# Decoder layer on one core: scatters paced by quarters, value bias prepared later, residual before the combine weights

## The reference

```
x = layernorm(x + attn(x))            # causal
x = layernorm(x + xattn(x, ctx))      # V = ctx @ Wv + bv, out = context @ Wo + bo
x = layernorm(x + moe(x))             # top 2 of 8, y = sum of weight * expert(x)
```

## Time and profile before

| | |
|---|---|
| median of 3 runs | 1257.66 us (1256.6 to 1260.25) |
| the profiled execution | 1263.13 us, its span 1261.4 us |
| PE busy | 1059.1 us (84% of the span) |
| DVE busy | 806.9 us (64%) |
| ACT busy | 580.3 us (46%) |
| POOL busy | 266.1 us (21%) |
| mean granted clock of PE | 0.922 of full speed |

### The profile page before, as it was taken

The page is one execution under the profiler, slowest core; times in us unless marked ns, Lnnn a source line. Parts: engine busy times, 40 slices in busy tenths (PEclk is TensorE's granted clock), DMA queues, the critical chain, the costliest instruction groups (busy, mean ns, idle before and its releaser), DMA issues.

```text
span 1261.4 us, 29339 instructions
## 1 busy us (share of the span) xinstructions
PE 1059.1 (84%) x10925; PEld 787.2 (62%) x10925; DVE 806.9 (64%) x1955; ACT 580.3 (46%) x937; POOL 266.1 (21%) x309
## 2 busy tenths in 40 slices
PE   4799999999988999997988899868439999999930
PEld 2465665656666666665656566545329999999920
DVE  3677787777788887776767676655534444444447
ACT  1366666666655565644436354545212222222214
POOL 1034222232222200002020201120422222222210
PEclk8899999999999999999898988888559999999975
DMA  6005635536440001001010100010147676777654
GB/s 260 27 28 176 197 125 175 172 117 206 141 117 28 11 18 44 10 10 45 10 45 10 46 11 23 16 37 2 58 134 213 209 219 210 217 214 212 203 225 195
DMA packets 94650, 139.27 MB, mean 110 GB/s; under 512 B 11217, under 2 KB 68945, under 8 KB 93105
## 3 DMA queue, kind: packets, MB, share of 16 engines
q1 hardware_dynamic: 87888, 114.98, 29.1%
q0 software_dynamic: 6624, 22.42, 4.6%
HBM read 76.56 MB, written 60.29 MB: 108 GB/s over the span
## 4 chain that ended last, share of the span: by engine, by line
PE 67%; DVE 17%; issue 8%; another core or an unknown queue 3%; ACT 2%; SPq 2%; DMA 2%; DVEq 0%; ACTq 0%; POOLq 0%
PE PS L814 10%; PE PS L825 10%; PE PS L551 9%; PE PS L572 8%; PE PS L521 6%; PE PS L629 4%; DVE part L1108 4%; PE PS L625 4%; PE PS L670 3%; PE PS L643 2%; PE PS L696 2%; PE PS L708 1%; PE PS L803 1%; PE PS L528 1%
## 5 line engine op out<-in xcount | busy, mean ns | idle before, releaser
L1108 DVE TENSOR_REDUCE part<-PS 128x6 f32<-128x768 f32 (+1 forms) x256 | 269.9, 1086 | 92.9 <-PE PS L528 59.8
L891 ACT ACTIVATE pT<-PS 128x768 f32<-128x768 f32 (+1 forms) x256 | 220.8, 915 | 111.8 <-PE PS L551 89.2
L551 PE MATMUL PS<-big 32*128 32x256 f32 (+1 forms) x2048 | 136.4, 380 | 21.0 <-issue 15.7
L572 PE MATMUL PS<-pT,vaug 128*32 128x256 f32 (+1 forms) x2048 | 129.3, 371 | 22.4 <-DVE y L1242 16.1
L1567 POOL TENSOR_SCALAR_AFFINE_SELECT pT<-pT 128x512 f32<-128x512 f32 x128 | 81.6, 638 | 311.4 <-ACT pT L891 307.3
L814 PEld LDWEIGHTS PS<-oT,big 128*128 128x128 f32 x1136 | 140.1, 194 | 5.4 <-ACT oT L1002 1.8
L814 PE MATMUL PS<-oT,big 128*128 128x128 f32 x1136 | 140.8, 278 | 1.0 <-ACT oT L1002 1.0
L551 PEld LDWEIGHTS PS<-big 32*128 32x128 f32 x2048 | 98.3, 189 | 65.0 <-issue 63.2
L825 PE MATMUL PS<-w2s,qkn 128*128 x568 | 134.4, 380 | 0.0
L902 ACT ACTIVATE oT<-PS 128x256 f32<-128x256 f32 x128 | 49.0, 383 | 174.9 <-PE PS L572 148.7
L1002 ACT ACTIVATE oT<-PS 128x256 f32<-128x256 f32 x71 | 27.2, 383 | 189.9 <-PE PS L803 189.9
(11 more groups left out here) (169 smaller groups left out, 1646.5 us busy)
## 6 DMA issues: line engine op xcount, KB each, us to landing
big<-w SPq DMA_DIRECT2D x71, 512.0 KB
xs_dram<-zrow SPq DMA_DIRECT2D x24, 1496.0 KB, 9.3
oT<-xs_dram SPq DMA_DIRECT2D x71, 136.0 KB
xin<-xT SPq DMA_DIRECT2D x16, 256.0 KB, 2.8
w2s<-w POOLq DMA_DIRECT2D x1, 4096.0 KB, 15.3
xb<-x SPq DMA_DIRECT2D x16, 256.0 KB, 11.3
xin<-ctxT SPq DMA_DIRECT2D x16, 256.0 KB, 2.8
big<-p_dram SPq DMA_DIRECT2D x4, 1024.0 KB, 7.9
```

The lines of the kernel that those rows point to most:

```text
L551: ins = pe.matmul(o, keys, a[r0:r1, 0, g, q0:T], start=True, stop=True)
L572: ins = pe.matmul(o[PADDED * i:PADDED * (i + 1), q0:T], vaug[:, n % 4, kt, head(g, i), :], pT[:, k % 2, i, kt * T:kt * T + T - q0], start= ...
L891: act.activation(pT[:, k % 2, 2 * half:2 * half + 2, 0:wide], src, ACT.Exp).then_inc((exp_a, exp_b)[half], 1)
L1108: dve.tensor_reduce(dst, src, AX.X, ALU.max, negate=True).then_inc((max_a, max_b)[half], 1)
```

## The change

1. `turn_bias` and `take_bias` move from q = 1 to q = 6, `fold_bias` from q = 2 to q = 7, `add_folded` from q = 5 to q = 8.
2. `residual` of a block moves from the start of the quarter r = 0 to the end of the quarter before it (r = 3), behind `lay_out` and ahead of `combine_weights`.
3. `scatter` on POOL waits, in every quarter in which PE computes scores, until the scores of that quarter are done, before it issues the quarter's two indirect DMAs.

```diff
@@ PE
                 if q == 0:
                     prepare_gains()
-                elif q == 1:
+                elif q == 6:
                     turn_bias()
-                elif q == 2:
+                elif q == 7:
                     fold_bias()
@@ DVE
                 if r == 0:
-                    residual(block_at(q, PROJECT_AT + 1))
                     take_ranks(routed_at(q, PLACE_AT))
...
                     lay_out(block_at(q, LAY_AT))
+                    residual(block_at(q, PROJECT_AT))
                     combine_weights(routed_at(q, RANK_AT))
                 if q == 0:
                     prepare()
-                elif q == 1:
+                elif q == 6:
                     take_bias()
-                elif q == 5:
+                elif q == 8:
                     add_folded()
@@ POOL, scatter
                     ends = nt * TOPK if q == QUARTERS - 1 else min(2 * j + 2, nt * TOPK)
+                    u = group_at(q, SCORE_AT)
+                    if u is not None:
+                        pool.wait_ge(scores_pe, NG * u[0] + u[1] + 1)
                     for c in range(2 * j, ends):
```

## The result

The median went from 1257.47 us (1256.6 to 1260.25, four runs) to 1218.47 us (1215.94 to 1220.28, four runs): ratio 0.9685, 95% interval 0.9662 to 0.9708. The profiled execution took 1220.28 us, its span 1218.5 us, granted clock 0.944.

A forecast was written before the change was run, and what follows sets the result against it. Bound by PE (67% of the chain) and DVE (17%), plus PE's start wait and late reports during scatter bursts. 1263.1 - 8.0 (start) - 33.5 (gate) + 3.6 (residual) = 1225.2 profiled, 1219.7 as median; range 1210 to 1245.

The forecast's parts named there:

- The late reports come with indirects in a row: Cross-attention, five batches: POOL's bursts of eight scatters hold PE's reports; bursts cost 38.5 us with the slower clock.
- B: Scatters: reports not held by the burst, or only in a profiled execution; gate saves nothing, 1253 us; chance 0.11.
- A: Paced scatters: each pair holds 1.6 us on the path in three quarters; gate saves 14.5, 1239 us; chance 0.12.
- C: Paced scatters: reports held in each of four quarters, 3 us a pair; slower, 1275 us; chance 0.05.
- The sum: Whole kernel: 1263.1 - 8.0 - 33.5 + 3.6 = 1225.2 profiled; 5.5 off for the median gives 1219.7 us.
- Size of the gate: Paced scatters in five batches: 6.7 us saved per batch, 33.5 in all; bounds 38.5 and 14.5.
- 7.7 us a burst: Quarters r = 1 and 2 with scatters: 7.7 us longer, some 5.4 late reports, the rest PE's clock at 0.50.
- The pairs: Paced scatters: nothing for four in a row in r = 0 and 1; 0.5 us each in r = 2 and 3.
- The start: Kernel start: PE's 8.99 us wait for late loads goes, first maxima at 31.4 instead of 39.76; 8.0 us saved.
- The residual: Routing quarters: residual ahead of `combine_weights` loses cover, 4 x 0.3 + 1.2 + 1.2 = 3.6 us; bounds 0 and 5.
- the two terms of 1.2: Residual, routing quarters at 831.89 and 881.91: combine weights no longer run while DVE waits; 1.2 us lost in each.
- The signs named: First maxima 31.4; paired scatters, no remote wait over 1.5 before 860, r = 1 and 2 together 15 to 16, clock near 1.00.

The follow-up runs named there:

- the first comparison: The whole change against the kernel before, four runs each: 1257.47 to 1218.47 us, ratio 0.9685.
- chips 6 and 8: Chip 6: change with one scatter a quarter, 1216.01 us (before 1258.33). Chip 8: moved bias, one scatter a quarter, residual in old place, 1218.35 (before 1260.37).
- chips 7, 2 and 9: Kernel before, unchanged: 1214.40 us on chip 7, 1220.90 on chip 2, 1219.11 on chip 9; parts, spacings and the whole change were run beside it.
- chip 9: The whole change against the kernel before: 1210.74 us beside 1219.11, ratio 0.9935; moved bias alone 1206.11, ratio 0.9912.
- chip 2: Kernel before, unchanged, 1220.90 us; whole change 1212.44, with one scatter a quarter 1211.28, with four in r = 0 and four in r = 2 1214.74.
- the residual alone: Only the residual moved behind `lay_out`, against the kernel before on chip 7: 1215.11 us, ratio 1.0018.
- the single scatters: Whole change with one indirect a quarter instead of two for batches ending with blocks 17 to 25: 1216.01 us on chip 6, 1211.28 on chip 2.

## Why the prediction was right, step by step

**The late reports come with indirects in a row**: right in the first comparison, on chips 6 and 8 too by their times and by the "remote" waits of the kernels run there, but only half of the story. On chips 7, 2 and 9 the same bursts delay nothing. The prediction took the 38 us for a property of the kernel. It weighed B at 0.11 and priced it at 1253; B's outcome came true in another form: on those three chips the gate is worth nothing, and the whole change 0.9935, 8 us. Had the comparison been made there, the forecast of 38 us less would have been wrong by 30. The forecast needed, without knowing it, a comparison where late reports are there, as in its trace; in that much it was lucky. B's other half, that only a profiled execution has the holds, does not fit: the four runs beside the profiled one took 1256.6 to 1260.25 too. Of rivals A and C neither appeared. What the record lacks is a part alone on a chip with late reports; that the gate and not another part gave the 30 us there is read from where the time went.

**The sum.** 1219.7 against 1218.47 is closer than its parts, and that is luck. The sum for the profiled execution was 1225.2, and it took 1220.28, 4.9 less. By q = 101 the gain was 11.3 instead of 8.0, and behind q = 134 another 1.5 came that no term has. The medians agree because 5.5 us were taken off for the distance of the profiled execution to the median; in the kernel after that distance is 1.8.

**Size of the gate.** The forecast was 33.5 less the residual's 3.6, so 29.9. From q = 101 to 134 the gain is (251.33 + 12.14) - (225.46 + 7.94) = 30.1; the residual's first 0.3 and second 1.2 fall outside this stretch, so 31.4 is what was forecast for it. Term by term: 7.7 us a burst held the late reports and something else. Without late reports the same burst of the kernel before takes 596.17 - 587.94 = 8.23 from r = 1 to r = 2, as a block without scatters does (511.05 - 502.82); by the table the bursts cost 27.6 / 4 = 6.9 and 7.2. The rest of the 7.7 is there without them too, in PE's clock. Three windows (us, busy time of PE, PEld, DVE, ACT and POOL, granted clock) over the stretch from the maxima of r = 2 to those of r = 3: the first batch in after, then the first and the second batch in after on chip 9:

```profile
584.09:591.98 7.89, 7.89 (x69) 5.14 (x69) 5.81 (x14) 3.87 (x6) 1.94 (x2) 0.81 0.15 48
```

```profile
586.50:594.49 7.99, 7.99 (x69) 5.17 (x68) 5.82 (x14) 3.86 (x6) 1.93 (x2) 0.79 0.17 49
644.29:650.72 6.43, 6.43 (x69) 4.56 (x68) 5.83 (x15) 3.87 (x6) 1.94 (x2) 1.00 0.20 59
```

The granted clock of 0.50 of the earlier trace rows is gone, but the 1.00 that was expected everywhere is about 0.8 in this stretch in some batches, which then takes 7.9 to 8.0 us against 6.43 in the earlier trace rows: in all four of the kernel after, in one of four in the same kernel on chip 9, and in two of four in the kernel before on chip 2. PE shows as busy the whole time in each. What lowers the clock in one batch and not in the next was not found. Nor does it decide the sum: on chip 9 other quarters were slow instead, so that the four batches took 224.95 us against 225.46.

**The pairs.** Nothing was taken for the four in a row of r = 0 and 1: right in the first four batches (8.28 us to the next maxima, against 8.23), wrong in the fifth, where the next scores need the result sooner: 7.94 against 4.97, 3 us. In r = 3, 0.5 was taken for a late report. The row that decides is another: 0.9 us of `add_bias` holding DVE's L1128. The prediction looked at `add_bias` when it asked what stands behind the waiting POOL, and cleared it since its result is needed three quarters on. It should have asked also what `add_bias` runs beside once it is moved. In r = 3 the late report itself (0.4) does not add to it, since the stretch takes 7.05 us with and without late reports. For r = 2, 0.5 was taken too; the stretch takes 8.0 us with late reports, as it does without them where the clock is as low, so none shows on the path.

**The start.** The steps on the path are within 0.4 us: heads scaled at 22.56 (22.8 predicted), transposes 22.62 (22.9), maxima 31.18 (31.4). Off the path, v of block 0 ran in 1.89 us and not 3.36, so that PE was done at 20.34 instead of 22.4, and then waited 2.28 for DVE. The gain to the first maxima is 8.58, predicted 39.76 - 31.4 = 8.4; `add_folded` behind them takes the 0.42 that were priced. No term has the wait for the second `xin`, which this execution did not meet and some others with the moved bias did (0.94 to 3.56 us). By q = 101 the lead has grown to 587.09 - 575.81 = 11.3, part of which are the 0.93 us of late report in the earlier trace rows; the rest wasn't separated. On its own the move gave 0.9925 and 0.9912, 9 to 11 us, on chips without late reports.

**The residual.** 0.3 in each of four routing quarters: from the maxima of q = 99 to those of q = 101 it takes 578.27 - 565.03 = 13.24 on chip 9 and in the residual alone 585.56 - 572.33 = 13.23, against 587.94 - 575.02 = 12.92 in the kernel before on chip 2. So 0.3, as said. First the residual alone, then before on chip 2:

```profile
572.33 2.36 DVE L1108 TENSOR_REDUCE part<-PS 128x4 f32<-128x1024 f32 x2 [0.16 <-PE PS L521]
...
585.56 2.36 DVE L1108 TENSOR_REDUCE part<-PS 128x4 f32<-128x1024 f32 x2 [0.19 <-PE PS L521]
```

```profile
575.02 2.36 DVE L1108 TENSOR_REDUCE part<-PS 128x4 f32<-128x1024 f32 x2 [0.16 <-PE PS L521]
```

The first of the two terms of 1.2 can be read as well: from the maxima of q = 131 to those of q = 132 it takes 800.03 - 792.72 = 7.31 us in the residual alone and 6.35 in the kernel before, on both chips, so 0.96. The second falls behind the last maxima and could not be told apart from noise. Together that is 4 x 0.3 + 1.0 = 2.2 us; the residual alone measured 1.0018, 2 us with an interval from -0.7 to 5.2, beside 3.6 predicted.

**The signs named.** "No remote wait over 1.5 us before 860" failed by its letter (3.7), since the limit was set without subtracting the wait that is there anyway. r = 1 and r = 2 together took 16.17 where 15 to 16 was said, and the granted clock near 1.00 was 0.81 in r = 2. The others held.

**What stays open.** Why some chips show late reports and others none. The program, the data and the pace of POOL's issue were the same. Whether it is the chip or something that changes with time was not tried: no chip was met twice in the experiments, the chip of the first comparison is not on record, and in order of time late reports were there in the first comparison, missing on chips 7, 2 and 9, and there again on chips 6 and 8. Nor is it known whether the issue of the indirects or their data delays PE's reports.

## What to carry to other kernels

Run the kernel before again, on another chip, before a gain is credited to a cause: the 30 us of the paced scatters were there in three comparisons and absent in three. When a transfer is paced, ask of every other instruction in that queue which operation of the neighbour engine it now runs beside; here a POOL addition behind a pair of indirects cost 0.9 us a batch by falling on a DVE operation of 0.16. When a kernel spaces work by a condition, look where the condition ends: four of the single scatters ran in a row there and brought the late report back. And subtract the wait that is there anyway before a wait is called the cost of something.

## What the hardware showed that was not expected

- The same program took 1257 to 1260 us where PE's reports come late during POOL's indirects (first comparison, chips 6 and 8) and 1214 to 1221 where they don't (chips 7, 2 and 9): 3%, none of it in the expert phase, which took 310.0 us with late reports and without.
- Where it happens, the hold grows with the indirects in a row: 0.4 us for two, 2.1 to 2.5 for four, 4.3 for eight, by the waits of ACT. For a single one it was nothing in r = 1 and 0.4 us in r = 3, where a POOL addition follows.
- A DVE operation of 128x2 elements took 1.89 us in place of 0.16 beside POOL's indirect and addition; one that began during the addition took 0.81.
- The start of the same code varies from run to run: first maxima at 30.39 to 36.40 us in kernels with the moved bias, with a load that landed late and matmuls of 6.77 us in place of 3.60.
